# A two-layer graph attention kernel: row sums by ScalarE's four-part copies, and aggregate steps interleaved with dot products

## The reference, cut to what matters

```python
h = relu(layernorm(x))
seq = (h @ W_seq).reshape(N, 16, 32)
scores = leaky_relu(seq@a1 [:, None] + seq@a2 [None, :]) masked by adj
x = x + elu(softmax(scores) @ seq @ W_out + b_out)
h = relu(layernorm(x))                                  # "h1" below
z = (h @ W_q.T + b_q) @ (h @ W_k.T + b_k).T / sqrt(512)
z = where(z * adj == 0, -10000, z * adj)
x = x + relu(softmax(z) @ (h @ W_v.T + b_v))
```

## Time and profile before

| | us |
|---|---|
| median of 3 runs | 452.01 |
| lowest, highest | 451.4, 453.9 |
| the profiled execution | 451.98 |
| its span, first to last instruction | 450.1 |
| TensorE busy | 393.3 (87%) |
| VectorE busy | 368.4 (82%) |
| GpSimd busy | 255.9 (57%) |
| ScalarE busy | 245.7 (55%) |

### The profile page before, as it was taken

The page is one execution under the profiler, slowest core; times in us unless marked ns, Lnnn a source line. Parts: engine busy times, 40 slices in busy tenths (PEclk is TensorE's granted clock), DMA queues, the critical chain, the costliest instruction groups (busy, mean ns, idle before and its releaser), DMA issues.

```text
span 450.1 us, 6244 instructions
## 1 busy us (share of the span) xinstructions
PE 393.3 (87%) x2058; PEld 281.5 (63%) x2070; DVE 368.4 (82%) x731; ACT 245.7 (55%) x511; POOL 255.9 (57%) x268
## 2 busy tenths in 40 slices
PE   7999999998799998999977997978998999968860
PEld 4888887786588886886554755645656855434430
DVE  3999999986899999998799999689854568989900
ACT  4379777783999999872442443343433346142220
POOL 2335151321868866876786535883524777788640
PEclk9599999999899999999996999989999999989995
DMA  8988999710000023435755432763212676679941
GB/s 322 395 347 316 380 313 350 272 50 25 4 6 6 7 29 91 103 112 151 232 155 148 151 95 87 208 208 112 95 47 96 193 207 200 200 171 130 127 61 19
DMA packets 26996, 70.02 MB, mean 156 GB/s; under 512 B 7892, under 2 KB 8148, under 8 KB 24788
## 3 DMA queue, kind: packets, MB, share of 16 engines
q0 software_dynamic: 13056, 38.45, 32.4%
q1 hardware_dynamic: 13904, 31.16, 19.0%
q10 hardware_dynamic: 4, 0.00, 0.0%
HBM read 52.47 MB, written 17.13 MB: 155 GB/s over the span
## 4 chain that ended last, share of the span: by engine, by line
POOL 28%; DVE 16%; issue 15%; PE 11%; DMA 2%; ACT 1%; DVEq 0%; POOLq 0%
PE psum L1349 7%; POOL s_shared L1271 7%; POOL s_shared L1300 5%; POOL out_dram L1284 4%; POOL s_shared L1252 3%; POOL s_rs L1282 3%; DVE s_shared L814 3%; DVE s_shared L812 3%; DVE s_shared L1044 3%; POOL s_x L1290 2%; POOL s_early L1300 2%; PE psum L1450 2%; DVE s_x L828 2%; DVE s_shared L821 1%; DVE h_t L1044 1%
## 5 line engine op out<-in xcount | busy, mean ns | idle before, releaser
L1101 ACT ACTIVATE s_shared<-psum,seq_all 128x320 bf16<-128x320 f32 x192 | 81.9, 571 | 6.0 <-PE psum L1349 4.3
L1349 PE MATMUL psum<-s_shared 128*128 128x198 bf16 x768 | 75.1, 254 | 9.6 <-POOL s_shared L1252 9.6
L1349 PEld LDWEIGHTS psum<-s_shared 128*128 128x128 bf16 x768 | 67.9, 98 | 17.4 <-POOL s_shared L1252 9.9
L563 PE MATMUL psum<-w_seq,hT 128*128 128x272 f32 x256 | 63.3, 402 | 0.4 <-ACT w_seq L424 0.4
L1371 PE MATMUL psum<-w_out,hT 128*128 128x512 f32 x128 | 61.4, 625 | 0.4
L563 PEld LDWEIGHTS psum<-w_seq,hT 128*128 128x128 f32 x256 | 49.0, 195 | 10.2 <-ACT w_seq L424 0.5
L1393 PE MATMUL psum<-w_qk,s_early 128*128 128x257 f32 x240 | 54.5, 379 | 0.0
L1393 PEld LDWEIGHTS psum<-w_qk,s_early 128*128 128x128 f32 x240 | 44.3, 189 | 6.0
L1271 POOL DMA_INDIRECT s_shared<-seq_dram,tab x30 | 37.4, 1246 | 11.3 <-issue 8.9
L1371 PEld LDWEIGHTS psum<-w_out,hT 128*128 128x128 f32 x128 | 26.2, 205 | 26.3 <-issue 25.4
L282 POOL TENSOR_TENSOR rstd<-veps,power 128x1 f32<-128x1 f32 x16 | 8.9, 558 | 54.9 <-DVE veps L468 54.9
(11 more groups left out here) (267 smaller groups left out, 742.1 us busy)
## 6 DMA issues: line engine op xcount, KB each, us to landing
adj_ring<-in_adj_dram SPq DMA_DIRECT2D x16, 1024.0 KB, 7.8
seq_dram<-seq_all POOLq DMA_DIRECT2D x16, 264.0 KB, 4.0
x_ring<-in_x_dram SPq DMA_DIRECT2D x16, 256.0 KB, 8.2
h_dram<-h_t SPq DMA_DIRECT2D x16, 256.0 KB, 2.3
w_seq<-in_L_gnn_W_seq_dram SPq DMA_DIRECT2D x1, 1024.0 KB, 5.5
w_q<-in_L_gnn_W_q_dram SPq DMA_DIRECT2D x1, 1024.0 KB, 13.5
w_k<-in_L_gnn_W_k_dram SPq DMA_DIRECT2D x1, 1024.0 KB, 15.7
w_v<-in_L_gnn_W_v_dram SPq DMA_DIRECT2D x1, 1024.0 KB, 8.6
```

Of the source, the lines that this page charges most:

```text
L563: last = pe.matmul(bank[2 + 2 * (t % 2) + i][:, 0:SX // 2], hT[:, t % 2, c * P:(c + 1) * P], w_seq[:, c, i * (SX // 2):(i + 1) * (SX // 2) ...
L1101: last = act.activation(ind[i][:, j, PAD:], bank[4 + i][:, 0:LN], ACT.Sign, bias=seq_all[:, j, D + n:D + n + 1])
L1349: last = pe.matmul(acc(i)[:, k, 0:3 * W2], ind[i][:, j, k * P:(k + 1) * P], rhs.rearrange("p t w -> p (t w)"), start=(j == 0 and k != 1), ...
```

## The change

Five things.

1. `accumulate` is gone. ScalarE copies each transposed tile of h1 in four parts of 128 columns, each with `accum_out`: this sums, for each feature, over the 128 nodes of the tile. VectorE adds up 16 columns per feature at the end (one small reduction), and TensorE makes the broadcast sum with four matmuls against `ident`, after the queries of place 12, which stood behind the sum before. h1 of tile 4 now has to be transposed and copied too.
2. In the first layer `norm_bias(k - 1)` stands behind `scores` in steps 4, 6 and 8, and behind the multiply of `aggregate(k + 2)` in steps 12 and 13.
3. In the second layer each step of an aggregate is followed by a dot of a later tile; the dots of tile 5 stand between the adds of tiles 11, 13 and 15. `add_row` waits for the add before it in its own tile.
4. At the end the adds of tiles 7 and 5 alternate.
5. The tables that place ScalarE's exponentials and bases change.

```diff
+HEAVY = [k for k in range(T) if SLOTS[SEQ[k]] > 1]
...
-EXP1_AT = {2: 1, 4: 2, 8: 3, 11: 4}
-BASES_AT = {0: (1, 2, 3), 1: (4,), 3: (5, 6, 7), 5: (8, 9), 9: (10, 11, 12), 10: (13,), 12: (14, 15)}
-WEIGHTS_AT = {0: 1, 3: 2, 5: 3, 9: 4, 12: 5}
+EXP1_AT = {2: 1, 3: 2, 7: 3, 12: 4}
+BASES_AT = {0: (1, 2, 3, 4), 2: (5, 6), 3: (7,), 5: (8, 9), 8: (10, 11), 9: (12, 13), 13: (14, 15)}
+WEIGHTS_AT = {0: 1, 2: 2, 5: 3, 8: 4, 13: 5}
...
-                def accumulate(t):
-                    dve.wait_ge(h1_done, t + 1)
-                    if t == 0:
-                        dve.tensor_copy(h_acc[:, :], h_t[:, 0, :]).then_inc(summed, 1)
-                    else:
-                        dve.wait_ge(summed, t)
-                        dve.tensor_tensor(h_acc[:, :], h_acc[:, :], h_t[:, t % 2, :], ALU.add).then_inc(summed, 1)
...
+                    behind = k >= 2 and k + 2 in HEAVY and k not in SCORES_AT and k - 1 not in SCORES_AT
+                    if k in SCORES_AT and k - 1 not in SCORES_AT and k > 2:
+                        scores(SCORES_AT[k])
+                        norm_bias(k - 1)
+                    elif not behind:
                         norm_bias(k - 1)
...
+                def aggregate_and_dot(t, u, lo=0, hi=TOP):
+                    hi = min(hi, SLOTS[u])
+                    for i in range(max(SLOTS[t], hi - lo)):
+                        if i < SLOTS[t]:
+                            add_row(t, i)
+                        if lo + i < hi:
+                            dot(u, lo + i, lo + i + 1)
...
+                dve.wait_ge(h1T_done, T)
+                dve.tensor_reduce(col_sum, col, AX_X, ALU.add).then_inc(summed, 1)
...
-                aggregate1(11)
-                dot(5)
-                aggregate1(13)
+                aggregate_and_dot(11, 5, 0, 3)
+                aggregate_and_dot(13, 5, 3, 6)
+                aggregate_and_dot(15, 5, 6, 8)
                 scores1(4)
-                aggregate1(15)
+                aggregate1(9)
                 normalise1(4)
-                aggregate1(9)
-                aggregate1(7)
-                aggregate1(5)
+                for s in range(SLOTS[5]):
+                    if s < SLOTS[7]:
+                        add_row(7, s)
+                    add_row(5, s)
...
-                    act.activation(h1T(t), bank[1], ACT.Copy).then_inc(h1T_done, 1)
+                    for c in range(C):
+                        last = act.activation(h1T(t)[:, c * P:(c + 1) * P], bank[1][:, c * P:(c + 1) * P], ACT.Copy,
+                                              accum_out=col[:, c, t:t + 1])
+                    last.then_inc(h1T_done, 1)
...
-                pe.wait_ge(summed, T)
+                queries(EARLY)
+                pe.wait_ge(summed, 1)
                 pe.wait_ge(hidT_done, T)
-                pe.matmul(bank[0], ones[:, 0:P], h_acc).then_inc(h_sum_mm, 1)
-                for t in range(EARLY, T - 1):
+                for c in range(C):
+                    last = pe.matmul(bank[0][:, c * P:(c + 1) * P], col_sum[:, c:c + 1].to_broadcast([P, P]), ident[:, :])
+                last.then_inc(h_sum_mm, 1)
+                for t in range(EARLY + 1, T - 1):
```

More of the change, by code:

```diff
@@ L740, in h1_no @@
         def h1_no(t):
-            return t + (t < NO_SLOT)
+            return t + 1
         def u_bank(t):
@@ L893, in aggregate @@
                     w = sc[:, o:o + K, :].unsqueeze(3).to_broadcast([P, K, H, DH])
-                    step(dve.tensor_tensor(rows, rows, w, ALU.mult))
+                    dve.tensor_tensor(rows, rows, w, ALU.mult).then_inc(weighed, 1)
+                    if tile is not None:
+                        norm_bias(tile)
+                    dve.wait_ge(weighed, HEAVY.index(k) + 1)
                     last = dve.tensor_tensor(hb, G(t)[:, 0, 0:D], G(t)[:, 1, 0:D], ALU.add)
@@ L971, in _ @@
                 aggregate(3)
[L972 to L976 removed]
+                for k in range(1, T + 1):
+                    residual(k - 1)
                     if k - 1 in SCORES_AT:
```

86 lines of the change are left out of this document (44 added, 42 removed).

## The result

The changed kernel takes 455.64 us (median of 8 runs, 454.37 to 457.05), the kernel before 452.79 us (median of 8, 451.4 to 453.9). The ratio is 1.0055, 95% interval 1.0035 to 1.0074: slower by 0.4 to 0.7%. The forecast was 453.3 us, in a range up to 456.4, with 0.38 for slower by over 0.5%. The profiled execution took 454.37 us with a span of 452.8, against 451.98 and 450.1 before. It is the fastest of its eight, so the two profiles differ by 2.4 us where the medians differ by 2.9.

What follows compares the result with a forecast made beforehand. VectorE bounds the first layer, then TensorE; 40 serial gathers and the work after the last follow. 451.98 - 4.4 (first layer ends earlier) + 5.7 (last transposes later after the gathers) = 453.3 us, range 448.7 to 456.4.

Steps and rivals of the forecast that it cites:

- The first term: First layer: ends 4.4 us earlier, bounds 3.0 and 5.3, moving the first gather from 347.0 to about 342.6 us.
- a first gather before 341 us: GpSimd's first gather, forecast near 342.6 us: one before 341 us would show the forecast wrong.
- From the variance to the bias it was 1.23 us: First layer, steps 4 to 7: GpSimd's answer takes 1.23 us, so steps 5 and 7 gain 0.3 us each.
- The 1.15 us each for steps 4 and 6: First layer: the next scores move ahead of norm_bias and cover GpSimd's answer, gaining 1.15 us per step, 2.3 together.
- From step 12 on TensorE has next to no gaps, so later savings (...) are worth nothing: Late first layer: four more removed sums and the multiply moved ahead of norm_bias in two steps gain nothing.
- The second term: Second layer, from T0 (last gathered tile, 5, complete) to the last transposes: 5.7 us later, bounds 1.8 and 6.9.
- that rival: Second layer: dot and add do not overlap, add holds VectorE 0.78 us; 454.3 us, chance inside the forecast's 0.43.
- the restarts: TensorE's products after two pauses in the second layer: 6.3 and 5.5 us at lower clock, together priced at 3.6 us.
- The rival of dearest restarts: Second layer: both TensorE restarts at slowest rows, position 11's transposes later than T0 + 9.4; 454.5 us, chance 0.27.
- Warm restarts: Second layer: TensorE restarts at full clock after both pauses and the first-layer gain stands; 449.4 us, chance 0.20.
- The sign "over 5 us": Before tile 5's first dot: VectorE waits over 5 us for a gather, if the forecast is right.
- From there to the end ... both stay: Behind the last transposes: 22.7 us to the span's end and 1.9 us outside the span stay unchanged.

Runs made afterwards that it cites:

- e7: Kernel before, each addition into the sum of normalised rows replaced by a one-input statistics instruction of equal length, sum left out: 451.33 us, ratio 0.9938.
- e8: Changed kernel with one ScalarE copy of each transposed tile instead of four with sums, column sums left out: 456.1 us, ratio to the kernel before 1.0047.
- e9: Changed kernel, gathers of tile 12 and later issued only once ScalarE has copied position 1: 462.23 us, ratio to the kernel before 1.0168.
- e10: e9 with adds of tiles 11, 13, 15 ahead of tile 5's first dot, and tile 7 before tile 5: 452.18 us, ratio to the kernel before 0.9948.
- e2: Kernel before with the changed kernel's second layer and tables: 491.37 us, ratio to the kernel before 1.0135.
- e1: Changed kernel with the old second layer and tables: 481.55 us, ratio to the kernel before 0.993.
- e4: Changed kernel with the bases of tiles 7 and 5 written behind position 12's copy instead of 13's: 481.64 us, no usable ratio in this first run.

## Right and wrong, step by step

**The first term was too small, beyond its bounds** (4.4 forecast, 3.0 to 5.3; 6.6 measured at the first gather, 7.06 at T0). One of the forecast's own signs of being wrong, a first gather before 341 us, came true. Two steps of it failed.

The first is "From the variance to the bias it was 1.23 us". I took GpSimd's power at the 0.95 us that the trace of before shows, and charged the additions only with two slow DMA issues (1.0 us). Without an addition beside it the power takes 0.56 us. In steps 5 and 7, where I had let GpSimd take its 1.23 us, the bias came 0.95 and 0.91 us behind the variance (249.47 to 250.42, 269.89 to 270.80). That is most of the 0.6 us by which the gain at step 8 was above the forecast: 4.0 (281.46 to 277.48, though the changed kernel came 0.3 us later into the loop) against 3.4. The 1.15 us each for steps 4 and 6 came in (1.19 and 1.24), and steps 8 to 10 gave 1.2 where 1.0 was forecast. The numbers for this stood in the trace of before: powers of 0.57 to 0.59 us in steps 1, 2, 9 and 10, where no addition overlapped them, and 0.86 to 0.96 elsewhere. I had read the rule of the Trainium skill, GPSIMD Engine Reference, section Key points, for the DMA issues alone. By that rule the power was exposed too, and `e7` agrees for both (0.56 instead of 0.95 us for the power, 0.95 instead of 1.45 for an issue).

The second is "From step 12 on TensorE has next to no gaps, so later savings (...) are worth nothing", with 0.4 us taken off for TensorE. From step 12 to the first gather the gain grew from 5.3 to 6.6 us. From variance 16 to the first gather it took 5.87 us before and 5.48 after, from variance 15 to variance 16 5.15 and 4.77: each shorter by the 0.4 us of the power. It stands on TensorE's own path there, because the transposes wait for h1, and h1 for the bias. TensorE at the transposes of the last two tiles of h1, before and then after:

```profile
338.48 0.66 PE L1380 MATMUL psum<-ident,h_t 128*128 128x128 f32 x4 [1.27 <-ACT h_t L1152]
...
343.64 0.66 PE L1380 MATMUL psum<-ident,h_t 128*128 128x128 f32 x4 [0.81 <-ACT h_t L1152]
```

```profile
332.26 0.66 PE L1401 MATMUL psum<-ident,h_t 128*128 128x128 f32 x4 [0.88 <-ACT h_t L1172]
...
337.03 0.66 PE L1401 MATMUL psum<-ident,h_t 128*128 128x128 f32 x4 [0.42 <-ACT h_t L1172]
```

Each wait is 0.39 us shorter; `e7` has the same 0.88 and 0.42. The other half of the growth from 5.3 to 6.6 us lies between steps 13 and 14, and its reason was not found.

**The second term was right in mechanism and nearly in size** (5.7 forecast, 6.6 measured, bounds 1.8 to 6.9). Tile 11 at T0 + 2.7, TensorE's pause, the base at 19.0 and position 14 at 25.1 all came within 0.5 us of the table. Add after dot held VectorE for 0.67 us (395.94 to 396.61), so that rival is out. What was mis-sized are the restarts. The first took 5.8 us instead of 6.3, the second 6.55 instead of 5.5, together 4.1 us more than two steps at full speed, where 3.6 were forecast. I had given the second the price of a row with 2.86 us idle, for a pause of 4.16. Other pauses between 3.8 and 4.8 us cost 5.6 (`e8`), 7.15 (`e9`) and 6.4 us (`e10`), so the value is not a function of the pause alone, and a range of 5.6 to 7.2 would have been fair. The rival of dearest restarts named T0 + 9.4 as its point, and position 11 came at 8.5: it did not happen. Yet the last transposes, at T0 + 31.6, came close to that rival's 31.9, because the second restart cost more than its 5.99 us. Warm restarts did not happen either.

I expected VectorE's wait before tile 5 at over 6 us; it was 4.25 there and 1.39 in front of tile 7's dots, since dot(7) had to wait too. The sign "over 5 us" was missed.

**"From there to the end ... both stay" was wrong.** 22.7 us became 25.9. All eleven traces with the new first layer have 25.9 to 26.4 us, the three without it (before, `e2`, `e7`) 22.7 to 23.0, whatever the chip. `e8` rules out the ScalarE copies.

The traces show where the 3.2 us lie. The timeline views leave branches out, but the recorded trace has them, and the last instruction of every trace is a closing branch of TensorE (`COMPARE_BRANCH`). It starts at 449.74 us before and at 449.30 after, 13.4 us behind the start of the last scatter in both (13.3 to 13.7 in all fourteen traces). Before, it lasts 0.40 us and ends the span at 450.14; after, it lasts 3.50 us and ends the span at 452.80. In the three traces with the old first layer it lasts 0.30 to 0.40 us, in the eleven with the new one 3.46 to 3.94. So 3.1 of the 3.2 us are this one instruction.

What it waits for can only be argued. In all fourteen traces a packet of 16 KB in an instruction queue starts 0.9 to 1.6 us after this branch. In the three, the branch is over by then, and the packet lies behind the span; in the eleven, the branch is still running. The DMA queues in the last 14 us of the span, before and then after:

```profile
q0 software_dynamic: 225, 0.40, 19.9%
```

```profile
q0 software_dynamic: 102, 0.18, 7.2%
q8 instruction: 1, 0.02, 0.5%
q14 instruction: 2, 0.02, 0.4%
```

That fits a branch that needs code which is not there yet with the new first layer. A second such packet follows in the eleven, 0.7 to 1.2 us after the branch is over, so it cannot be what the branch waits for. TensorE's own program grew too: its recorded instructions, matmuls apart, are 2236 in the eleven traces and 2225 in the three. No run changed TensorE's program alone, so why the branch takes longer stays open.

Of the measured slowdown of 2.4 us between the two profiled executions, this piece is larger than the whole: without it the profiled execution would have been 0.8 us faster than before, which is within the bound of no change. It would also take the medians from 2.9 us apart to nearly even.

**So the forecast was near for reasons that partly cancel.** Span: -7.06 + 6.60 + 3.16 = +2.7 us; forecast -4.4 + 5.7 + 0 = +1.3. The forecast said slower, and slower it was, but that is luck: without the closing branch, a term that was not in the sum, the two others come to -0.5 us.

## What to carry to other kernels

- Before an instruction that waits for a late transfer is put between two that do not, look at who waits for the second. The adds of three tiles, but for the first add, stood behind such a wait in `e9`; with all nine ahead of it in `e10` the next engine was 6 to 7 us earlier, although VectorE's total work is the same.
- An instruction's duration in a trace can contain another engine's. Compare it where the neighbour is absent (0.57 to 0.59 against 0.95 us here) before it goes into a sum, and look for it on every chain that it is part of.
- Take the piece behind the last computation into the list of terms, and compare it first when two traces are laid side by side. Instructions that a view leaves out can fill it: here one branch took 3.50 instead of 0.40 us.

## What the hardware showed beside that

**GpSimd's small instruction ended 0.43 us after VectorE's large one, whatever its length.** The changed kernel puts the power beside the multiply of two steps. VectorE and GpSimd in step 12 and 13 of the changed kernel:

```profile
309.43 1.22 DVE L896 TENSOR_TENSOR s_shared<-s_shared,s_sc 128x1024 f32<-128x1024 f32 x1
...
309.60 1.47 POOL L1304 TENSOR_TENSOR s_rs<-s_ve,power 128x1 f32<-128x1 f32 x1 [3.71 <-DVE s_ve L921]
```

```profile
315.10 1.75 DVE L896 TENSOR_TENSOR s_shared<-s_shared,s_sc 128x1536 f32<-128x1536 f32 x1
...
315.28 2.00 POOL L1304 TENSOR_TENSOR s_rs<-s_ve,power 128x1 f32<-128x1 f32 x1 [2.49 <-DVE s_ve L921]
```

A power on 128x1 values takes 1.47 and 2.00 us here, where alone it takes 0.56. It ends 0.42 and 0.43 us after the multiply (310.65 and 316.85), and beside an addition of 0.69 us (314.71 to 315.40 before) it ended at 315.83, 0.43 us after it too. So it is not slowed in proportion: whichever two-input instruction it overlaps, some 0.43 of its 0.56 us come behind that instruction's end. Moving the bias behind the multiply therefore hides little of the power: VectorE still waits 0.46 us for it (bias at 311.11), as it did behind the addition, against 0.69 us in steps 14 to 16, where nothing stands between (322.99).

**ScalarE's pause on two chips.** ScalarE in `e1` (a copy of u, then the copy of position 1), and GpSimd in the same stretch:

```profile
369.44 0.39 ACT L1138 ACTIVATE seq_all<-psum 128x257 f32<-128x257 f32 x1 [13.52 <-remote]
...
391.92 0.60 ACT L1219 ACTIVATE bout_bc<-psum 128x512 f32<-128x512 f32 x1 [21.83 <-remote]
```

```profile
385.65 0.95 POOL L1320 DMA_INDIRECT s_early<-h_dram,s_near_rank  x1 [0.30 <-issue]
...
394.19 1.16 POOL L1320 DMA_INDIRECT s_shared<-h_dram,s_near_rank  x1 [7.58 <-DVE h_t L1046]
```

What ScalarE copies at 391.92 had been ready since 358.3. In six of the eight traces the pause ends 5.8 to 6.8 us after the last of the 40 gathers. In `e1`, where GpSimd had to stop at 385.65 with four to go, it ends 6.3 us after that stop. In `e4` it ends 3.2 us after the last gather, and a second pause of 2.2 us brings it to 6.0. No instruction packet shows between 355 and 395 us in `e1`, where the changed kernel's trace has two between 370 and 375. That fits code of ScalarE that gets no turn while gathers run, and `e9` was made to test it, but no kernel with the break in the gathers has run on such a chip. It stays a guess.
